# Windowed attention in six layers: probabilities times the shifted inputs and a product Wv Wo, with new engine orders

## The reference, cut to what matters

```python
HEADS, DIM_HEAD, WINDOW, DEPTH = 16, 64, 32, 6
def attn_layer(x, Wqkv, qs, ksc, Wo):        # x is shift_tokens(x): the second half of the features, one token later
    q, k, v = jnp.split(x @ Wqkv, 3, -1)     # 1024 columns each
    q, k = l2norm(q) * qs, l2norm(k) * ksc   # per head
    q = q * cos * scale + rotate_half(q) * sin * scale
    k = k * cos / scale + rotate_half(k) * sin / scale
    # each window of 32 queries sees its own 32 keys and the 32 before them
    attn = softmax(where(mask, -max, q @ look(k).T * 8.0))
    return (attn @ look(v)).reshape(b, n, 1024) @ Wo
def ffn_layer(x, g, bln, W1, b1, W2, b2):    # also of shifted x
    a, gate = split(layernorm(x) * g + bln) @ W1 + b1
    return a * gelu(gate) @ W2 + b2
for i in range(DEPTH):
    x = attn_layer(shift_tokens(x), ...) + x
    x = ffn_layer(shift_tokens(x), ...) + x
```

## Time and profile before

| what | us |
|---|---|
| median of 3 runs (2148.30 to 2151.88) | 2149.88 |
| span of the profiled execution | 2143.9 |
| PE busy | 2022.6 (94%) |
| DVE busy | 1497.0 (70%) |
| POOL busy | 1522.5 (71%) |
| ACT busy | 1286.6 (60%) |

### The profile page before, as it was taken

One profiled execution on the slowest core, in us unless ns is written; L12 is line 12 of the kernel. 1 busy time (PEld: TensorE's weight loads), 2 busy tenths in 40 slices (PEclk: granted clock), 3 DMA queues, 4 the chain that ended last, 5 costly groups with the idle time before them and its releaser, 6 DMA issues.

```text
span 2143.9 us, 84229 instructions
## 1 busy us (share of the span) xinstructions
PE 2022.6 (94%) x35763; PEld 1356.1 (63%) x35763; DVE 1497.0 (70%) x2268; ACT 1286.6 (60%) x1844; POOL 1522.5 (71%) x2307
## 2 busy tenths in 40 slices
PE   4789999878999999999999999999999999999997
PEld 1455555545666667666766667666676666766675
DVE  2445454458877887777877787777877788778773
ACT  3567777634656665665656565566656666566653
POOL 3344444458878887788877778778887788777880
PEclk8899999998999999999999999999999999999998
DMA  4999999932323222242222422224222242222221
GB/s 125 289 347 355 344 357 344 348 126 61 74 62 111 68 65 65 63 113 67 72 62 62 113 62 69 65 62 120 63 66 62 63 117 70 62 62 63 68 72 43
DMA packets 120004, 261.51 MB, mean 122 GB/s; under 512 B 29092, under 2 KB 34128, under 8 KB 118864
## 3 DMA queue, kind: packets, MB, share of 16 engines
q1 hardware_dynamic: 119632, 256.13, 41.4%
HBM read 87.06 MB, written 68.29 MB: 72 GB/s over the span
## 4 chain that ended last, share of the span: by engine, by line
PE 68%; POOL 4%; DVE 3%; issue 2%; ACT 1%; POOLq 0%; DVEq 0%; ACTq 0%
PE ring L463 22%; PE ring L529 9%; PE ring L473 8%; PE yps L541 7%; PE ring L499 7%; PE ring L569 5%; PE ring L510 4%; PE tpose L579 3%; PE ring L491 1%; POOL roped L275 1%; DVE turned L643 1%; PE tpose L551 1%; DVE ss L652 1%; DVE stats L701 0%; POOL ss L248 0%
## 5 line engine op out<-in xcount | busy, mean ns | idle before, releaser
L643 DVE TENSOR_TENSOR turned<-ring,ropes 128x1024 f32<-128x1024 f32 x384 | 452.0, 1219 | 303.0 <-PE ring L463 303.0
L240 POOL TENSOR_TENSOR roped<-turned 128x512 f32<-128x512 f32 x384 | 522.5, 1386 | 170.4 <-PE ring L473 169.0
L463 PE MATMUL ring<-wqkv,xT 128*128 128x512 f32 x1152 | 567.4, 616 | 5.2 <-ACT xT L328 4.0
L275 POOL TENSOR_TENSOR roped<-roped,rnorm 128x1024 f32<-128x1024 f32 x192 | 361.5, 1904 | 7.5
L1170 POOL TENSOR_SCALAR less<-less,lowest 128x512 f32<-128x512 f32 x256 | 175.3, 697 | 240.0 <-DVE lowest L1139 240.0
L1139 DVE CUSTOM_DVE_ANT_0 less<-ps_b,shifted 128x512 f32<-128x512 f32 x256 | 166.6, 688 | 226.0 <-PE ps_b L1002 79.7
L463 PEld LDWEIGHTS ring<-wqkv,xT 128*128 128x128 f32 x1152 | 198.2, 192 | 161.0 <-issue 149.8
L369 ACT COPY pT<-ring 128x1024 f32<-128x1024 f32 x96 | 97.2, 1012 | 305.8 <-PE ring L510 305.8
L529 PEld LDWEIGHTS ring<-pT,vwin 64*64 64x64 f32 x12288 | 198.5, 134 | 51.9 <-issue 51.5
L317 ACT ACTIVATE squares<-ring 128x1024 f32<-128x1024 f32 x192 | 197.3, 1028 | 55.8 <-DVE turned L643 55.8
L529 PE MATMUL ring<-pT,vwin 64*64 64x32 f32 x12288 | 219.7, 220 | 4.9 <-issue 3.4
(11 more groups left out here) (133 smaller groups left out, 3234.7 us busy)
## 6 DMA issues: line engine op xcount, KB each, us to landing
vwin<-v SPq DMA_DIRECT2D x1536, 64.0 KB, 2.0
shifted<-scratch_w SPq DMA_DIRECT2D x64, 1024.0 KB, 12.6
scratch_w<-wrows SPq DMA_DIRECT2D x48, 1026.0 KB, 10.9
scratch_w<-x SPq DMA_DIRECT2D x16, 1026.0 KB, 10.4
wqkv<-in_l_wqkv SPq DMA_DIRECT2D x6, 1536.0 KB, 6.9
wo<-in_l_wo SPq DMA_DIRECT2D x6, 512.0 KB
...
```

The lines of the kernel that those rows point to most:

```text
L240: nc.gpsimd.tensor_tensor(halves[2][:, :, side, :], halves[0][:, :, side, :], halves[1][:, :, 1 - side, :], ALU.add).then_inc(s[name + "_a ...
L275: nc.gpsimd.tensor_tensor(whole, whole, norm, ALU.mult).then_inc(s[name + "_roped"], 1)
L463: last = nc.tensor.matmul(out[:, half, :], xT[:, t % SEQT * P:(t % SEQT + 1) * P], wqkv[:, layer_of(t), at + half * 512:at + (half + 1) * ...
L643: ins = nc.vector.tensor_tensor(turned[:, n, part, :].rearrange("p (h d) -> p h d", d=DH), heads, table, ALU.mult)
```

## The change

The attention of a layer is rewritten: since attn @ (x Wv) @ Wo is (attn @ x) @ (Wv Wo), head by head, the values are no longer made.

- project V, the array v and its 16 DMAs a tile are gone. Instead xs holds the shifted x of a tile, by token, in 3 places, and beside it the same moved by 32 tokens (the window before); 5 DMAs a tile make them (windows).
- attend is now eight matmuls of 32 rows, 128 columns of weights and 512 moving columns (16 heads by 32 queries): four windows with their own tokens, then four with the tokens before, the four of one kind on the four row groups of the array and into four PSUM banks. Its result is 1024 columns in OA and 1024 in OB, which two copy_o bring to SBUF.
- project_out is sixteen matmuls with wvo, the 128x128 product Wv Wo of each head, in two halves of eight.
- wvo is made once a layer: turn_wv (8 transposes), copy_wv, make_wvo (16 matmuls of 64 rows), two copy_wvo; the weights arrive in 13 DMAs a layer instead of 8.
- turn_p leaves PE and copy_p leaves ACT: DVE turns the probabilities by one instruction in 32x32 blocks, behind divide.
- Q and K are freed in PSUM by rotate instead of square (FREED), the scores lie in ring 0 like K, square waits for the projection and rotate for square. hidden stands in step 1 instead of 0, project_ffn in 2 instead of 1, turn_xn in 1 instead of 3, offsets in step 0 and normalise at the end of step 0.
- All lists are in a new order; scores and attend are no longer halved. roped has a second place.

The diff, cut to its core:

```diff
-        wqkv = sb("wqkv", [P, 2, 3 * INNER])
-        wo = sb("wo", [P, 2, PAIRS, D])
+        NX = 3
+        wqk = sb("wqk", [P, 2, 2 * INNER])
+        wv = sb("wv", [P, INNER])
+        wo = sb("wo", [P, PAIRS, D])
+        wvT = sb("wvT", [P, PAIRS, P])
+        wvo = sb("wvo", [P, 2, 2, PAIRS, D])
...
+        xs = sb("xs", [P, NX, 2, D])
...
+        pT = sb("pT", [P, 2, HEADS, W])
+        oT = sb("oT", [P, HEADS, P])
...
+        ROOM = {"K": 0, "QT": 1, "XT": 4, "H0": 1, "H1": 2, "H2": 0, "OA": 1, "OB": 2, "XS": 3, "F": 3, "KT": 2, "S": 0, "Q": 1,
+                "XN": 3, "Y": 4, "T": 1, "M0": 1, "M1": 2}
+        FREED = {"Q": ("q_rotated",), "K": ("k_rotated",), "QT": ("qT_copied",),
+                 "KT": ("kT_copied",), "S": ("scores_taken",), "OA": ("oa_copied",), "OB": ("ob_copied",),
                  "H": ("gelu_made", "h_ready"), "XT": ("xT_copied",), "XN": ("xnT_copied",), "XS": ("xn_made",), "Y": ("y_added",),
-                 "F": ("x_done",)}
+                 "F": ("x_done",), "T": ("wvT_copied",), "M": ("wvo_copied",)}
...
+                half, here, before = D // 2, t % TILES, (t - 1) % TILES
+                a, b = t % NX, (t - 1) % NX
+                if t < TILES:
+                    sp.wait_ge(s["normed"], t + 1)
+                elif t % SEQT == 0:
+                    sp.wait_ge(s["x_done"], t // SEQT - BATCH + 1)
+                at_least(sp, s["o_summed"], t - NX + 1)
+                at_least(sp, prev_in[(t - NX + 1) % NX], PREV * ((t - NX + 1) // NX + 1) if t >= NX else 0)
+                sp.dma_start(xs[:, a, 0, 0:half], x[:, here, 0:half]).then_inc(s["own_in"], 16)
+                sp.dma_start(xs[1:P, a, 0, half:D], x[0:P - 1, here, half:D]).then_inc(s["own_in"], 16)
+                first = zero[P - 1:P, :] if t % SEQT == 0 else x[P - 1:P, before, half:D]
+                sp.dma_start(xs[0:1, a, 0, half:D], first).then_inc(s["own_in"], 16)
+                sp.wait_ge(s["own_in"], OWN * (t + 1))
+                sp.dma_start(xs[W:P, a, 1, :], xs[0:P - W, a, 0, :]).then_inc(prev_in[a], 16)
+                sp.dma_start(xs[0:W, a, 1, :], xs[P - W:P, b, 0, :]).then_inc(prev_in[a], 16)
...
                 step, g = n % SEQT, n // SEQT
-                norms(n - 2)
-                scale(0, n - 2)
-                scale(1, n - 2)
+                add(0, n)
+                add(1, n)
+                norms(n)
+                scale(0, n)
+                scale(1, n)
+                if step == 3:
+                    deviations(g - 1)
                 if step == 1:
                     add_b2(g - 2)
-                add(0, n - 1)
-                add(1, n - 1)
-                if step == 0:
-                    deviations(g - 2)
                 if n >= 0 and n % (SEQT * BATCH) == 13:
                     make_ropes(n // (SEQT * BATCH) + 1)
...
-                    act.wait_ge(s[name + "_rotated"], t + 1)
+                    act.wait_ge(s[name + "_made"], t + 1)
...
+                    at = W2 if kind == "OB" else 0
+                    nc.scalar.copy(oT[:, :, at:at + W2].rearrange("c h (b q) -> c b h q", q=W),
+                                   ring[:, room(kind), :, :].rearrange("c b (h q) -> c b h q", q=W)
+                                   ).then_inc(s["oa_copied" if kind == "OA" else "ob_copied"], 1)
...
                 step, g = n % SEQT, n // SEQT
-                if step == 0:
-                    normalise(g - 2)
-                copy_p(n - 3)
-                if step == 0:
+                copy_x(n + 2)
+                square(1, n)
+                if step == 1:
                     copy_xn(g - 2)
-                square(0, n)
-                exps(n - 2)
                 copy_q(n - 1)
-                square(1, n)
-                if step == 0:
+                copy_k(n - 1)
+                copy_wv(product_layer(n, 2))
+                copy_wvo(product_layer(n, 1))
+                if step == 1:
                     gelus(g - 2, 0)
                     gelus(g - 2, 1)
                     gelus(g - 2, 2)
-                copy_k(n - 1)
-                copy_o(n - 3)
-                copy_x(n + 2)
-                copy_v(n)
+                copy_o("OA", n - 2)
+                copy_o("OB", n - 2)
+                square(0, n + 1)
+                exps(n - 1)
+                if step == 0:
+                    normalise(g - 2)
...
+            def make_wvo(layer):
+
+                if layer is not None:
+                    pe.wait_ge(s["wvT_copied"], layer + 1)
+                    for half in range(2):
+                        out = take("M", layer, half)
+                        for j in range(half * PAIRS // 2, (half + 1) * PAIRS // 2):
                             for r in range(2):
+                                rows, at = slice(r * DH, (r + 1) * DH), j % (PAIRS // 2) * D
+                                last = nc.tensor.matmul(out[:, r, at:at + D], wvT[rows, j, :], wo[rows, j, :], start=True, stop=True)
+                        last.then_inc(s["wvo_made"], 1)
...
+            def attend(t):
+
+                if live(t):
+                    pe.wait_ge(s["p_turned"], t + 1)
+                    pe.wait_ge(prev_in[t % NX], PREV * (t // NX + 1))
+                    outs = (take("OA", t), take("OB", t))
+                    for own in (1, 0):
+                        for win in range(WT):
+                            rows = slice(W * win, W * win + W)
+                            last = nc.tensor.matmul(outs[win // 2][:, win % 2, :], xs[rows, t % NX, 1 - own, :],
+                                                    pT[rows, own, :, :].rearrange("p h q -> p (h q)"),
+                                                    start=own == 1, stop=own == 0, skip_group_check=True)
+                    last.then_inc(s["o_summed"], 1)
+
+            def project_out(t, half):
+
+                if live(t):
+                    if half == 0:
+                        pe.wait_ge(s["oa_copied"], t + 1)
+                        pe.wait_ge(s["ob_copied"], t + 1)
+                        pe.wait_ge(s["wvo_copied"], 2 * (t // (SEQT * BATCH) + 1))
+                        take("Y", t)
+                    out = view("Y")
+                    for h in range(half * PAIRS, (half + 1) * PAIRS):
+                        r, j = h // PAIRS, h % PAIRS
+                        last = nc.tensor.matmul(out[:, 0:D], oT[:, h, :], wvo[:, layer_of(t), r, j, :],
+                                                start=h == 0, stop=h == HEADS - 1)
...
                 step, g = n % SEQT, n // SEQT
+                turn_x(n + 2)
                 project("K", n)
+                if step == 1:
+                    turn_xn(g - 2)
+                project_out(n - 3, 0)
                 turn_qk(0, n - 1)
-                turn_x(n + 2)
-                if step == 0:
+                turn_qk(1, n - 1)
+                turn_wv(product_layer(n, 2))
+                make_wvo(product_layer(n, 1))
+                if step == 1:
                     hidden(g - 2, 0)
                     hidden(g - 2, 1)
                     hidden(g - 2, 2)
-                attend(n - 3, 0)
+                if step == 2:
+                    project_ffn(g - 2)
                 if step == 3:
                     shift(g - 1)
-                if step == 1:
-                    project_ffn(g - 2)
-                turn_qk(1, n - 1)
-                attend(n - 3, 1)
-                project("V", n)
-                scores(n - 1, 0)
+                project_out(n - 3, 1)
+                attend(n - 2)
+                scores(n - 1)
                 project("Q", n + 1)
-                scores(n - 1, 1)
-                turn_p(n - 2)
-                if step == 3:
-                    turn_xn(g - 1)
-                project_out(n - 3)
...
-                    dve.wait_ge(s[name + "_made"], t + 1)
+                    dve.wait_ge(s[name + "_squared"], t + 1)
...
+            def turn_p(t):
+
+                if live(t):
+                    dve.wait_ge(s["p_normed"], t + 1)
+                    at_least(dve, s["o_summed"], t)
+                    nc.vector.transpose(pT[:, :, :, :], probs[:, t % 2, :, :].rearrange("p h (o k) -> p o h k", k=W)
+                                        ).then_inc(s["p_turned"], 1)
...
-                if step == 2:
-                    add_ffn(g - 2)
-                rotate(0, n)
-                take_max(n - 2)
-                take_scores(n - 2)
-                add_y(n - 4)
+                sum_probs(n - 2)
+                invert(n - 2)
+                divide(n - 2)
+                turn_p(n - 2)
+                sum_squares(0, n)
                 rotate(1, n)
+                sum_squares(1, n)
+                if step == 0:
+                    offsets(g - 2)
+                add_y(n - 3)
                 if step == 3:
                     statistics(g - 1)
-                sum_probs(n - 2)
-                invert(n - 2)
-                sum_squares(0, n)
-                if step == 0:
```

(10 more changed lines are left out.)

214 lines of the change are left out of this document (85 added, 129 removed).

## The result

| | before | after |
|---|---|---|
| median, us | 2149.09 | 2356.29 |
| runs | 2143.15 to 2151.88 | 2347.41 to 2364.01 |
| span of the profiled execution | 2143.9 | 2352.6 |

The change makes the kernel slower: ratio 1.0965, 95% interval 1.0933 to 1.0998. The forecast was 2395 with a range of 2250 to 2480. The direction and most of the waits came as forecast. One of the two steps laid to DVE is mostly set by POOL, at the same length, and two large terms of the sum were off in opposite directions and hid some of each other.

A forecast was written before the change was run, and what follows sets the result against it. PE's matmuls bound the kernel before, 68.2 us a group; afterwards waits make it 78.5. 22 groups x 10.3 = 227, +9 for the first two, +12 for wvo: +248, span 2392, forecast 2395 us, range 2250 to 2480.

The forecast's parts named there:

- step 1: Take_max-to-take_max interval of a group where PE stops for normalise and gates: 26.0 us, 27.7 if the clock falls again.
- step 0: Take_max-to-take_max interval of a group, the plain DVE cycle with divide caught for 0.8 to 1.2: 16.0 us.
- the two steps laid to DVE: The intervals step 0 and step 3 of a group, whose pace DVE was to set: 16.0 and 16.7 us.
- PE's own work: PE's matmuls and transposes per group: 4.5 us less, 63.7 instead of 68.2.
- The forecast's cycle: DVE's loop per tile from take_max through rotate(1) to the scores, which wait for K's ring: 15.2 us.
- step 3: Interval where divide waits 0.5 and sum_squares(1), add_y and the statistics stand ahead of take_max on DVE: 16.7 us.
- Divide against POOL: DVE's divide waits for POOL's second scale or add nearly every time, for 0.5 to 1.8 us.
- step 2: Interval where a table load delays copy_x and so project_out, then PE's chain sets the pace: 19.0 us.
- the failed term: In step 1, a lowered PE clock after the stop before turn_xn: 1.7 us charged for such a stop.
- better overlap: Rival: divide isn't caught, the clock doesn't fall; 74.7 or 71.9 us a group, 2250 to 2320; chance 0.20.
- Start and tail: First two groups +9 us, some 4 us at the start for wvo; last two groups' feed-forward parts 0.
- faster: PE stays the bound: Rival: waits fall under other engines' work, PE's 63.7 us a group sets the time, 2054 us; chance 0.07.

The follow-up runs named there:

- e2: Changed kernel with DVE's transposition of the probabilities (turn_p) done twice per tile: 2404.2 us, ratio 1.1205.
- e1: Changed kernel with divide's product with rinv replaced by an in-place DVE transposition that reads the same array alone: 2326.2 us, ratio 1.0845.
- e9: Changed kernel with gates, offsets and normalise, copy_x and first normalisations moved earlier, plus rotate(1) ahead of sum_squares(0): 2213.7 us, ratio 1.0326.
- e3: Changed kernel with the three gates ahead of add_y in DVE's list instead of behind it: 2305.9 us, ratio 1.0758.
- e7: Changed kernel with the first normalisations of sequences 1 to 3 run ahead of the first period: 2339.3 us, ratio 1.0916.

## Why the prediction was right, and where it wasn't

**PE's own work: right, partly by luck.** 63.5 to 63.6 a group, forecast 63.7. But the forecast took the 4.5 off the group's length of 68.2, and PE's work before was 67.5: it fell by 3.9. attend's eight products take 2.00 (forecast 2.16); the row groups overlap. Two halves of project_out take 3.9, where 1.79 + 1.79 was forecast.

**DVE's steps: the lengths right, the way right in part.** The interval of step 0 is 16.05 against a forecast of 16.0 (15.2, and 0.8 for a caught divide). The forecast's cycle, scores behind rotate(1), sets nine groups of 21: 14.7 to 15.0 with a divide of 1.4, and 15.97 with a divide of 2.95, plus 1.7 once for the clock. In the other twelve it is 16.05 by another way: divide comes first, and POOL's second scale waits. The prediction saw that "6.8 against 6.95 decides whether divide slips in ahead of the second scale", but gave POOL's delay no price; that both cases cost the same 1 us is luck. e2 shows that these groups don't wait for DVE's work, e1 that they wait for POOL's. In step 3 DVE's own list is the bound, as the forecast has it, and e2 shows that. e9 shows the closed cycle in step 0 once POOL's scale isn't late.

**The transposition: right.** 1.2 forecast, 1.245 measured. It was never caught by POOL in 74 cases (1.245 to 1.247).

**Divide against POOL: right in kind and nearly in size.** Mean 1.83, forecast "near 2". By steps, medians: 2.10 in step 2, 1.98 in step 3, 1.24 in step 0, 1.42 in step 1. So it is caught in every tile of steps 2 and 3 of these groups and free in twelve of 21 in step 0, where POOL is caught instead. e1 puts the price at 0.7 in step 3 and 1.0 in step 0.

**The stops in step 1: right in place, one of them over-sized.** attend stood for 1.79 (forecast 1.9), and e3 recovers it: 1.83. turn_xn stood for 1.93, not 2.3, and behind that the clock fell in 3 groups of 22, not in each. This is the failed term: I charged 1.7 us a group for the clock, from one stop of 2.03 in the earlier trace rows. The price of one fall was right, since step 1 takes 25.7 with one and 24.05 without; how often it falls was not, and the kernel lost 8.7 us over twenty groups, 0.4 each. So step 1 is 24.05 instead of 26.0. Step 2 is 18.13 instead of 19.0: turn_qk's two halves take 1.75 in one go, not 2.1, and attend 1.93, not 2.15. Step 3 is 16.06 instead of 16.7. With layer changes and the few falls of the clock the mean group is 75.3, not 78.5. From group 2 to the last take_max the change costs 157 us, where my terms give 235 (22 x 10.3 and some 8 for wvo): -77.

The size landed near the "better overlap" rival (74.7 a group), by half of its mechanism: the clock mostly didn't fall, and step 1 is near its 24.3. Divide was caught in steps 2 and 3, though, and where it was free step 0 was no shorter. (The rival's second sum, 71.9, is 71.5 by its own terms.)

**Start and tail: wrong, too small.** The first group takes 78.6 (58.7 before), the second 76.3 against 68.2. That is +28, where I had 13. What was missing is first_norm caught by POOL; e7 gives 10.7 of it back. And the second group isn't one of tiles only, as I had it: its first turn_xn is at 645.8. The tail, forecast "0", is +15.5: from the last take_max to the end it is 57.6 us, against 42.1. Before, the last but one feed-forward part had its hidden ahead of that point. Now it lies behind, with a bare wait:

```profile
2301.17 1.09 PE L587 MATMUL tpose<-ident,xn 128*128 128x128 f32 x4 [6.28 <-ACT xn L413]
2305.46 6.12 PE L596 MATMUL ring<-xnT,w 128*114 128x512 f32 x12
```

"The last two groups' feed-forward parts run alone before and after: 0" was the false sentence: I had moved hidden by a step in the steady state and not at the end.

**The sum, as measured** from the two profiled executions, +208.7: 7.7 ahead of the first scores (hardly the change's, see above), 28.0 in the first two groups, 152.4 in the 21 after them, 5.1 in the last three intervals, 15.5 behind the last take_max. Against the forecast's +248 that is -77 in the groups, +15 at the start, +15 at the tail and +8 by chance.

**The rival "faster: PE stays the bound"** had named its own condition, scores that don't wait for rotate(1), with a step 1 under 22. e9_early comes close to it, with 20.8 in step 1, but steps 3 and 2 are still 16.5, and 70.2 a group isn't 68. None of these kernels beats the one before (2213.7 against 2144.2, ratio 1.0326). What stays open is whether the rest, 6.6 us a group above PE's 63.6, can be had: k and the scores in rings of their own would open the cycle, which wasn't tried, as no ring is free. By e9 it would gain nothing in step 3, since DVE's own list fills that step.
